# Absolute sums, layernorm statistics and next weight splits moved into the first attention, the first feed-forward rows moved beside the last key and value tiles

## What is computed

```python
x = x + L0_xattn(layernorm(x), ctx)     # stage 1 of this text: attention over ctx and x
x = x + L0_ffn(layernorm(x))            # stage 3: ternary ("bit linear") feed-forward
x = x + L1_xattn(layernorm(x), ctx)     # 16 heads; its keys and values are made in stage 2
x = x + L1_ffn(layernorm(x))            # routed experts

def bit_linear(x, w, b):
    gamma_x = clip(max(abs(x), axis=-1), 1e-5)
    x_dq = clip(round(x * 127 / gamma_x), -128, 127) / (127 / gamma_x)
    gamma_w = clip(mean(abs(w)), 1e-5)          # needs the whole matrix first
    w_dq = clip(round(w / gamma_w), -1, 1) * gamma_w
    return einsum('bsd,hd->bsh', x_dq, w_dq) + b
gate = silu(bit_linear(x, gate_w, gate_b)); val = bit_linear(x, val_w, val_b)
out = bit_linear(gate * val, out_w, out_b)      # hidden width 2048

k = rmsnorm((ctx @ Wk + bk) per head, kn_w);  v = ctx @ Wv + bv    # of L1_xattn
```

## Time and profile before

| | us |
|---|---|
| median of 3 runs | 1871.54 |
| lowest and highest | 1871.28 and 1875.71 |
| the profiled execution | 1874.65 |
| span of its trace | 1872.9 |
| stage 1 in the trace | 0 to 310.7 |
| stage 2 | 310.7 to 455.05 |
| stage 3 | from 455.05 |

### The profile page before, as it was taken

One profiled execution on the slowest core, in us unless ns is written; L12 is line 12 of the kernel. 1 busy time (PEld: TensorE's weight loads), 2 busy tenths in 40 slices (PEclk: granted clock), 3 DMA queues, 4 the chain that ended last, 5 costly groups with the idle time before them and its releaser, 6 DMA issues. The chain is left out here.

```text
span 1872.9 us, 26972 instructions
## 1 busy us (share of the span) xinstructions
PE 1752.1 (94%) x9950; PEld 1449.3 (77%) x9970; DVE 1237.4 (66%) x2357; ACT 852.0 (45%) x1621; POOL 558.8 (30%) x408
## 2 busy tenths in 40 slices
PE   6999996884799989999999999999889999999999
PEld 6988995763344458888888888888756789999876
DVE  4444433776789857677777767778666567676655
ACT  3222321674455545455555445555332256555411
POOL 2111111221666632122221212221120145464342
PEclk9999998997899998999999999999989999999999
DMA  6110113464122374122221212220053288888573
GB/s 224 34 34 22 34 45 109 153 223 145 23 68 70 88 208 145 57 93 90 89 80 57 79 57 86 95 68 1 1 193 116 88 279 277 281 279 269 194 251 107
DMA packets 160946, 225.38 MB, mean 120 GB/s; under 512 B 41655, under 2 KB 101303, under 8 KB 158647
## 3 DMA queue, kind: packets, MB, share of 16 engines
q1 hardware_dynamic: 150940, 189.50, 30.5%
q0 software_dynamic: 9888, 34.35, 5.8%
HBM read 171.65 MB, written 43.78 MB: 115 GB/s over the span
## 5 line engine op out<-in xcount | busy, mean ns | idle before, releaser
L1065 POOL TENSOR_TENSOR a_rq<-a_ssq,a_qhalf 128x4 f32<-128x4 f32 x64 | 65.1, 1017 | 404.2 <-DVE a_ssq L1374 404.2
L1212 ACT ACTIVATE a_pT_hi<-bank 128x512 fp32r<-128x512 f32 x128 | 69.5, 598 | 185.4 <-PE bank L1614 185.4
L78 PE MATMUL bank<-a_xT_hi,a_wq_lo 128*128 128x512 f32 (+1 forms) x384 | 144.7, 377 | 6.8 <-issue 3.7
L1206 ACT ACTIVATE a_scores<-a_scores,a_nmax 128x256 f32<-128x256 f32 x256 | 127.2, 504 | 27.5 <-DVE a_nmax L1389 27.3
L79 PE MATMUL bank<-a_xT_lo,a_wq_hi 128*128 128x512 f32 (+1 forms) x384 | 139.0, 362 | 0.0
L80 PE MATMUL bank<-a_xT_hi,a_wq_hi 128*128 128x512 f32 (+1 forms) x384 | 138.8, 362 | 0.0
L78 PE MATMUL bank<-a_wo_hi,a_oT_lo 128*128 128x512 f32 x320 | 127.1, 397 | 3.1 <-DVE a_oT_lo L416 1.5
L79 PE MATMUL bank<-a_wo_lo,a_oT_hi 128*128 128x512 f32 x320 | 125.3, 391 | 0.0
L1382 DVE SCALAR_TENSOR_TENSOR a_scores<-bank,a_rq,a_mask 128x256 f32<-128x256 f32 x256 | 106.1, 477 | 28.7 <-PE bank L80 20.4
L80 PE MATMUL bank<-a_wo_hi,a_oT_hi 128*128 128x512 f32 x320 | 125.0, 391 | 0.0
L1924 POOL TENSOR_TENSOR e_wg_lo<-raw_g,e_wg_hi 128x1408 fp32r<-128x1408 f32 x26 | 91.3, 3511 | 112.8 <-ACT e_wg_hi L1991 112.8
(11 more groups left out here) (404 smaller groups left out, 5350.5 us busy)
## 6 DMA issues: line engine op xcount, KB each, us to landing
raw_g<-in_egw SPq DMA_DIRECT2D x26, 704.0 KB, 4.8
raw_u<-in_euw SPq DMA_DIRECT2D x26, 704.0 KB, 6.2
a_xT_hi<-x1T_hi SPq DMA_DIRECT2D x16, 1024.0 KB, 6.0
a_xT_lo<-x1T_lo SPq DMA_DIRECT2D x16, 1024.0 KB, 8.3
raw_d<-in_edw SPq DMA_DIRECT2D x26, 512.0 KB, 5.7
y_routed<-m_y SPq DMA_DIRECT2D x39, 256.0 KB, 6.8
raw_d<-in_edw SPq DMA_DIRECT2D x26, 192.0 KB, 6.6
a_cTraw<-in_ctxT SPq DMA_DIRECT2D x8, 512.0 KB, 3.5
```

The source lines that it names most:

```text
L78: pe.matmul(out, w[1], x[0], start=first, stop=False)
L1065: pool.tensor_tensor(rq[:, h % HG, :], ssq[:, h % HG, :], qhalf[:], ALU.pow).then_inc(s_rq, 1)
L1206: act.activation(row, row, ACT.Exp, bias=nmax[:, i % 2, t:t + 1], accum_out=den[:, i % 2, t:t + 1]).then_inc(s_exp, 1)
L1212: act.activation(pT[b].hi[:], ptb[b][:].rearrange("p (k s) -> p k s", k=QT), ACT.Copy).then_inc(ft.hi, 1)
```

## The change

- **Stage 1** becomes straight code on all engines (no `Fori`). In turns 0 to 5 SP also loads the 24 chunks of the three matrices, 4 per turn, into the two `wraw` buffers that the weights of stage 1 have left (`piece`), and ACT takes the absolute sums (`absolute`, 4 per turn). DVE makes the statistics that stage 3 wants of the rows added a turn before (`next_statistics`). In the last turns POOL makes the gate rows, PE one product for all three means, DVE the three inverses, and ACT and POOL split `wk`, `wv` and the first two context tiles of stage 2. The context for stage 2 is loaded ahead of the chunks, and SP's loads of `cTraw` and `craw` for a turn now stand behind the 4 chunks of the turn before.
- **Stage 2** starts its products at once for the two context tiles that are ready. The chunks are loaded a second time (ring of 8) and rounded, two for each tile from 1 to 12. `normed` writes into `ksq`, and the transposes and `keys_out` lag by two tiles instead of one. Only the last two row tiles' statistics are made here. After tile 12 DVE makes `norm` of rows 0 to 3, `largest` and `scales`, ACT two `round_x` and DVE two `quantised_x`. POOL no longer waits for the stores at the end.
- **Stage 3** starts with the transposes of row tiles 0 and 1. The wait for the stores is on SP, ahead of the first load of keys.

Its core (the same sums and formulas in new places are left out):

```diff
 @ attention0, sync
+            for i in range(B):
+                if i:
+                    sp.wait_ge(s_cTlo, i)
+                    sp.dma_start(cTraw[:], ctxT_dram[:, :, i * S:(i + 1) * S]).then_inc(s_cT, 16)
+                    sp.wait_ge(s_clo, i)
+                    sp.dma_start(craw[:], ctx_dram[:, i * QT:(i + 1) * QT, :]).then_inc(s_c, 16)
+                for n in range(i * PER, min((i + 1) * PER, PIECES)):
+                    if i:
+                        sp.wait_ge(s_abs, n - PER + 1)
...
+                    piece(n)
+                if i * PER == PIECES:
+                    sp.wait_ge(s_abs, PIECES)
+                    sp.dma_start(grow, gb_dram.partition_broadcast(NR)).then_inc(s_grow, 16)
+                    sp.dma_start(wraw[0][:], wv1_dram).then_inc(s_wv1, 16)
 @ attention0, gpsimd
+            gate_rows()
             context(B - 1)
+            pool.wait_ge(s_kvhi, 1)
+            pool.tensor_tensor(kv.wk.lo[:], ahead.raw[:], f32(kv.wk.hi[:]), ALU.subtract)
+            next_context(0)
+            pool.wait_ge(s_kvhi, 2)
+            pool.tensor_tensor(kv.wv.lo[:], wraw[0][:], f32(kv.wv.hi[:]), ALU.subtract)
+            next_context(1)
 @ attention0, scalar
+            def absolute(n):
+                w, c = n // keep.chunks, n % keep.chunks
+                if n < PIECES:
+                    act.wait_ge(s_piece[n % PER], n // PER * 16 + 16)
+                    act.activation(pieces[n % PER], pieces[n % PER], ACT.Abs,
+                                   accum_out=keep.asum[:, w, c:c + 1]).then_inc(s_abs, 1)
 @ attention0, vector, between pT.lo and keys
+                if i:
+                    next_statistics(i - 1)
 @ keys_values_ternary
-        measured = {0: (0, range(0, 3)), 1: (0, range(3, 6)), 2: (0, range(6, 8)), 6: (1, half(0)), 7: (1, half(4)),
-                    11: (2, half(0)), 12: (2, half(4))}
-        averaged = {3: 0, 8: 1, 13: 2}
-        rounded = {4: (0, half(0)), 5: (0, half(4)), 9: (1, half(0)), 10: (1, half(4)), 14: (2, half(0)), 15: (2, half(4))}
+        rounded = {t: range(2 * t - 2, 2 * t) for t in range(1, PIECES // 2 + 1)}
 @ keys_values_ternary, sync
+            def piece(n):
+                w, c = n // NCH, n % NCH
+                after(sp, s_min, n - RING + 1)
 @ keys_values_ternary, gpsimd
             store(B - 1)
-            for j in range(2):
-                pool.wait_ge(s_st[j], B // 2 * 32)
 @ keys_values_ternary, vector
-            dve.wait_ge(s_whi, 1)
-            dve.tensor_tensor(wk.lo[:], ahead.raw[:], f32(wk.hi[:]), ALU.subtract).then_inc(s_wlo, 1)
+            last_statistics()
...
+                if t == T - 3:
+                    dve.wait_ge(s_rstd, 1)
+                    for j in range(PREP):
+                        norm(j)
+                if t == T - 2:
+                    largest()
+                    scales()
+            quantised_x(0)
+            quantised_x(1)
+            values_out(T - 1)
 @ keys_values_ternary, tensor
             def keys(t):
-                pe.wait_ge(s_clo, t + 1)
+                after(pe, s_clo, t + 1 - READY)
 @ ffn0_attention1, vector and sync
-            norm(0)
-            largest(0)
-            scales(0)
-            quantised_x(0)
-            for t in range(1, 4):
-                norm(t)
-            largest(1)
-            scales(1)
-            quantised_x(1)
-            dve.wait_ge(s_b, 32)
+            for s in stored:
+                sp.wait_ge(s, B // 2 * 32)
```

More of the change, by code:

```diff
@@ L342, in _ @@
             values(0)
-            with act.Fori(0, B - 1) as i:
+            for i in range(B - 1):
                 turn(i, True)
+            act.wait_ge(ahead.raw_loaded, 16)
+            act.wait_ge(q.mm, 2 * B)
+            act.activation(kv.wk.hi[:], ahead.raw[:], ACT.Copy).then_inc(s_kvhi, 1)
+            act.wait_ge(s_wv1, 16)
+            act.wait_ge(k.mm, 2 * B)
+            act.activation(kv.wv.hi[:], wraw[0][:], ACT.Copy).then_inc(s_kvhi, 1)
             turn(B - 1, False)
@@ new lines, in keys_values_ternary @@
+        mem = Region(nc, keep.base)
+        kst, vst = mem.take("kv_kst", [P, 2, G, S]), mem.take("kv_vst", [P, 2, QT, D])
+        kf = [mem.take(f"kv_kf{j}", [P, G, HD]) for j in range(2)]
+        ksq = [mem.take(f"kv_ksq{j}", [P, G, HD]) for j in range(2)]
+        bk = mem.take("kv_bk", [P, D])
+        assert mem.offset <= keep.area
+        mem = Region(nc, keep.area)
+        ring = [mem.take(f"kv_ring{j}", [P, CH]) for j in range(RING)]
+        assert mem.offset <= keep.high
+        mem = Region(nc, kv.end)
@@ L629, in _ @@
-            for b in (2, 3, 4):
-                context(b)
-            for c in half(0):
-                chunk(1, c)
-            context(5)
-            for c in half(4):
-                chunk(1, c)
-            for b in (6, 7):
-                context(b)
-            for c in range(NCH):
-                chunk(2, c)
+            piece(0)
+            piece(1)
+            context(2)
+            for n in range(2, RING):
+                piece(n)
+            context(3)
+            for n in range(RING, PIECES):
+                piece(n)
+                if n >= 10 and n % 4 == 2:
+                    context(n // 4 + 2)
@@ new lines, in round_x @@
+            def round_x(t):
+                act.wait_ge(s_sx, 1)
+                act.activation(prep.xn[:, t, :], prep.xn[:, t, :], ACT.Identity, bias=magic[:],
+                               scale=prep.sx[:, t:t + 1]).then_inc(s_xr, 1)
+            context_hi(READY)
+            act.wait_ge(s_const, 1)
+            for t in range(T):
+                cs = rounded.get(t, range(0))
+                squares(t)
+                for n in cs[0:1]:
+                    scaled(n)
+                root(t)
+                if t == 0:
+                    act.wait_ge(s_mv, QT)
+                    act.activation(std[:], mv[:, :, 1], ACT.Sqrt, bias=eps[:]).then_inc(s_std, 1)
+                if t >= 2:
+                    keys_out(t - 2)
+                for n in cs[1:2]:
+                    scaled(n)
```

656 lines of the change are left out of this document (340 added, 316 removed).

## The result

The changed kernel takes 1839.9 us (median of 4 runs, 1838.38 to 1842.28) against 1871.41 for the kernel before (4 runs): ratio 0.9829, 95% interval 0.981 to 0.9847. The profiled execution of before (1874.65) lay 3.2 us above its median, that of the changed kernel (1840.23) at its median, so between the two traces there are 34.4 us.

What follows compares the result with a forecast made beforehand. Stage 1 was taken as bound by PE, stage 2 by nothing for its whole length. About 15 us from the end, 7 from the start and 17 from tiles made 39 us saved: median 1832.5, range 1822 to 1844.

Steps and rivals of the forecast that it cites:

- Stage 1, costed at nothing: Stage 1: the added sums, statistics, loads and splits fit beside PE's work; 0 us, with up to 10 us kept for sums.
- The step's worry: Stage 1, turn 0: two absolute sums on ACT, 2.8 us, barely fit the 3.0 us of slack before PE takes `pT.lo`.
- Start of stage 2: Stage 2's start: first product at about 311.0 instead of 316.26, saving 5.3 us plus 4.1 of `wv.lo`, less 2.
- The clock's share: Stage 2's start: PE comes out of the barrier's idle at clock 0.50, losing 2 us.
- Tiles 1 to 12: Stage 2: 6.5 us per tile with two chunks, one meeting with POOL each; bias of tile 13 at 400.5.
- PE paces: Stage 2 rival: DVE's two chunks hide wholly, step 5.97 us, saving 47 us, 1825; chance 0.13.
- The end: Tiles 13 to 15 up to the first gate product: 24.7 us, plus 1.1 for store buffers, giving 426.4.
- The same work: Stage 3 from its first gate product on: the work is unchanged, so no time is gained or lost there.
- Both chunks meeting POOL: Stage 2 rival: each of a tile's two chunks collides with POOL, tile 7.3 us, saving 30, 1842; chance 0.11.
- The transfers: Stage 2 rival: reloaded chunks or K stores make tiles wait, 7.3 us or more, saving 27 to 30, 1843; chance 0.08.
- Stage 1 exposed: Stage 1 rival: 10 us of the sums lie on PE's path, saving 29, 1842; chance 0.04.
- slower than before: Stage 1 rival: all sums and statistics delay PE, stage 46 us longer, kernel 7 us slower, 1878.5; chance 0.04.

Runs made afterwards that it cites:

- doubled sums: Changed kernel with each of the 24 absolute sums of stage 1 done twice: 1840.10 us, ratio 0.981 to 0.985.
- the last two experiments on the start: Changed kernel with first two context tiles split in stage 2: 1841.52 us; changed kernel with first bias step waiting for bk's load alone: 1837.89 us.
- no context lo: Changed kernel with POOL's stage 2 subtraction for the context's lo part cut to one column of 128: 1833.28 us, ratio 0.975 to 0.980.

## Why the prediction came out as it did

**Stage 1, costed at nothing: right.** It ends at 310.90 (before: 310.74), though its first instruction comes at 2.20 instead of 3.60. With doubled sums nothing moved. A sum cost 1.06 us and its read 0.20, 30 us for the 24, not 34. The step's worry, 2.8 us in a slack of 3.0, was counted twice over: the second sum stands behind `pT.hi`, so only one of them delays it. `pT.lo` ends at 52.78 and PE takes it at 54.82:

```profile
51.49 1.29 DVE L526 TENSOR_TENSOR a_pT_lo<-bank,a_pT_hi 128x512 fp32r<-128x512 f32 x2 [1.78 <-ACT a_pT_hi L415]
54.82 0.28 PE L78 MATMUL bank<-a_pT_hi,a_V_lo 128*128 128x256 f32 x1
```

**Start of stage 2: the times right, the reason wrong.** First product 310.94 (forecast 311.0), bias of tile 1 at 322.46 (322.5). But the sum's remark that the start gives 7 us does not fit its own marks: the bias of tile 1 moved by 15.6. And PE's earlier product is not what set it: that mark hangs on the landing of small loads, as the last two experiments on the start show. The prediction gives no sum for 322.5, and its start has no such wait, so the hit is luck. The clock's share was sized well: the granted clock was 0.50 (1.2 GHz) from the barrier to about 314 us, and PE's first tile took 7.0 us where the second took 5.4, so 1.6 us against the forecast's 2.

**Tiles 1 to 12: right.** 6.46 us against 6.5. The collision is there, one per tile, 0.98 us against the 0.90 taken from the earlier trace rows, on the other instruction of the chunk. What set the pace was DVE, with the meeting as its price. The rival "PE paces" had the right floor, 5.97 against 5.93 (no context lo), but the changed kernel does not reach it: PE runs at 5.93 per tile only up to tile 8, where it has used up its lead, and at 6.37 to 6.49 behind it, waiting for `values_out` to empty its bank.

**The end: the step that was mis-sized.** From the bias of tile 15 to the gate product the forecast had 3.5 + 5.6 + 2.4, and 1.1 for stores: 12.6 us; it took 15.4. (The forecast's terms add up to 24.7 and it goes on with 24.8; the slip is 0.1.) The term of 5.6, "the last transposes ... and the barrier", took the wait for the last store to be gone, and 4.1 of those 5 us stayed, inside the barrier. The 1.1 for stores was nothing: in the changed kernel no instruction of DVE or ACT waits for a store. That the bias of tile 15 came 1.4 us before its forecast (412.31 against 413.7) covers half of it: the gate product was 1.3 us late. The preparation was said to be part of the 15 us gained at the end; it was moved, not hidden, and gained nothing (104.61 against 105.2). With it back in stage 3 the way from the bias of tile 13 to the gate product is 27.1 us, and it was 41.4 before. So what was gained there has another source, most likely the chunks that tiles 14 and 15 no longer round; no run put these back alone.

**Behind it: not foreseen.** From the gate product to the end the trace of before has 1407.6 us and the changed kernel 1410.8; the traces of all its variants have between 1410.3 and 1413.6. About 2 us come at the first queries of the second attention, where PE waits 5.7 us and not 3.7 (5.0 to 6.3 in the other traces); about 1 of them is made up behind it. Another 1.8 lie in the last turn of that attention, where the granted clock was 0.50 for 7 us (1308 to 1315) and 0.76 in the 7 us of before that answer to it. In the second trace of the changed kernel this turn is as short as before (20.9 us, against 22.8), so that part is not the change's. What makes the wait at the queries longer was not tried, and there is one trace of before only: this stays open. "The same work" took 3 us more.

**The sum.** 37.6 at the gate product, 3.2 given back, 34.4 between the traces; and 2.9 of it because before's profiled execution lay 3.2 above its median and the changed one's 0.3: 31.5. The forecast subtracted its 39 from either.

**The rivals.** Both chunks meeting POOL did not happen: the first chunk has 0.69 and 0.43 in each tile. The transfers did not run dry: DMA was busy for 0.67 of the stage, and neither ACT nor DVE waited for a chunk. Stage 1 exposed, and with it "slower than before", fell with the doubled sums.

## What to carry to other kernels

Work beside a bound engine is free as long as each queue's slack at the hand-over holds, not because the engine is idle on average: find the instruction that the bound engine takes next, and count only what stands ahead of its maker. A step moved into the neighbouring stage gains only if the engine that does it isn't the pace there; time both ends of the stretch. And where a wait is taken out ahead of a barrier, ask what else that engine has under way: here the issue of the last store had to leave POOL before the time came back. Read a floor from the engine that is never idle: the steps of another one can be shorter for a dozen tiles while it catches up.

## What the runs showed of the hardware that was not expected

- Behind POOL's issue of a transfer the barrier opened 1.6 us after the transfer had landed (4.1 to 4.4 us after the issue began), with no wait in the program; behind SP's it opened 1.31 us after the end of the issue and 2.5 us before the landing.
- A bf16 instruction of DVE from SBUF to SBUF goes from 0.43 to 1.42 us beside a subtraction on POOL of 1.3 us; instructions of 0.68 us with an input in PSUM are not touched by the same.
- Small loads of 0.5 KB behind larger ones landed 7.3 us after the barrier, later than the end of PE's first 12 products (with DVE waiting for one load alone, its bias behind them came at 4.4).
- Nearly the same stage 1 took 306 to 310 us from one trace to the next, more than several of the edits are worth; stretches between marks inside a trace told apart what the medians could not.
